# First feed-forward in three rounded parts, in halves of 256 rows, with its weights split on chip

## What the kernel must compute

```python
x = x + _L0_xattn_ref(_layernorm(x), ctx, w_in, b_in, w_out, b_out, w_ct, b_ct, 64)  # banded, 8 heads of 8
x = x + _L0_ffn_ref(_layernorm(x), w_r, b_r, w1, b1, w2, b2)
x = x + _L1_xattn_ref(_layernorm(x), ctx, ctx, Wq, Wk, Wv, Wfc, bfc)                 # 32 heads, 8 key groups
x = x + _L1_ffn_ref(_layernorm(x), gate_w, up_w, down_w, expert_weight, ln_gamma, ln_beta)

def _L0_ffn_ref(x, w_r, b_r, w1, b1, w2, b2):        # the part that is changed
    scores = einsum('bld,d->bl', x, w_r) + b_r
    _, idx = top_k(scores, l // 2)                   # the better half of each sequence's rows
    x_sel = take_along_axis(x, idx[:, :, None], axis=1)
    h = gelu(einsum('bkd,df->bkf', x_sel, w1) + b1)  # 256 -> 1024
    out_sel = einsum('bkf,fd->bkd', h, w2) + b2      # 1024 -> 256
    return zeros_like(x).at[batch, idx].set(out_sel)
```

## Time and profile before

| | |
|---|---|
| time, 3 runs | 342.03 us median (340.19 to 342.74) |
| the profiled execution | 341.85 us, span of the trace 340.1 us |
| busy share of the span | PE 92%, PEld 71%, DVE 70%, ACT 59%, POOL 53% |
| tile 7 of the banded attention | 138.75 to 153.70 us |
| first feed-forward, first half of rows, and last row choice | 164.20 to 185.46 us |
| second half, up to the first score pair | 185.46 to 207.45 us |
| granted PE clock in these stages | 1.00 of the full 2.4 GHz |

### The profile page before, as it was taken

One profiled execution on the slowest core, in us unless ns is written; L12 is line 12 of the kernel. 1 busy time (PEld: TensorE's weight loads), 2 busy tenths in 40 slices (PEclk: granted clock), 3 DMA queues, 4 the chain that ended last, 5 costly groups with the idle time before them and its releaser, 6 DMA issues.

```text
span 340.1 us, 7216 instructions
## 1 busy us (share of the span) xinstructions
PE 312.5 (92%) x2178; PEld 242.9 (71%) x2178; DVE 237.7 (70%) x921; ACT 199.9 (59%) x415; POOL 181.1 (53%) x294
## 2 busy tenths in 40 slices
PE   6978999999999999999998998869899999999993
PEld 5877667767676767765587886657567678888892
DVE  7878888999999998984426256754788746661264
ACT  4648887878787778768540324465768963113210
POOL 6648565677777856576604513343342822335643
PEclk9999999999999999999999999989999999999997
DMA  7999020201010101100000000000000000000000
GB/s 200 369 368 318 3 48 2 49 1 48 3 41 8 33 18 27 26 0 4 2 0 0 2 0 0 2 0 1 2 1 2 0 2 0 3 31 15 18 31 31
DMA packets 13301, 14.51 MB, mean 43 GB/s; under 512 B 2512, under 2 KB 11984, under 8 KB 13264
## 3 DMA queue, kind: packets, MB, share of 16 engines
q1 hardware_dynamic: 12688, 13.72, 12.9%
q10 hardware_dynamic: 576, 0.33, 0.3%
HBM read 10.64 MB, written 1.05 MB: 34 GB/s over the span
## 4 chain that ended last, share of the span: by engine, by line
PE 63%; DVE 16%; issue 8%; ACT 7%; POOL 5%; POOLq 0%; DVEq 0%; ACTq 0%
PE S L421 6%; PE S L761 6%; PE O L448 5%; PE ST L432 4%; DVE masked L1283 4%; PE ST L786 4%; PE S L555 4%; PE S L637 2%; PE S L704 2%; PE PJ L681 2%; PE O L718 2%; PE O L586 2%; PE PJ L394 2%; PE PJ L384 2%; PE XB L693 2%
## 5 line engine op out<-in xcount | busy, mean ns | idle before, releaser
L1283 DVE CUSTOM_DVE_ANT_0 masked<-S,band 128x192 bf16<-128x192 f32 x256 | 80.4, 354 | 12.7 <-PE S L421 11.6
L882 ACT ACTIVATE ex<-ST 128x384 f32<-128x384 f32 x128 | 61.4, 490 | 13.5 <-PE ST L432 11.8
L1067 POOL TENSOR_SCALAR rstd<-mv 128x1 f32<-128x1 f32 x40 | 12.0, 301 | 80.0 <-DVE mv L1220 79.9
L421 PE MATMUL S<-qk 128*128 128x384 f32 x128 | 53.2, 416 | 0.2
L432 PE MATMUL ST<-qk 128*128 128x192 f32 x256 | 47.7, 269 | 2.1 <-ACT ex L882 1.8
L432 PEld LDWEIGHTS ST<-qk 128*128 128x128 f32 x256 | 44.9, 189 | 4.4 <-issue 3.4
L421 PEld LDWEIGHTS S<-qk 128*128 128x128 f32 x128 | 24.1, 188 | 17.9 <-issue 16.1
L1127 POOL TENSOR_SCALAR_AFFINE_SELECT ex<-ex 128x512 f32<-128x512 f32 x32 | 21.3, 665 | 29.0 <-ACT ex L882 28.9
L448 PE MATMUL O<-ex,v 128*32 128x192 f32 x512 | 34.1, 338 | 0.0
L1414 DVE TENSOR_REDUCE mw<-S 128x8 f32<-128x512 f32 x32 | 22.0, 686 | 14.6 <-PE S L637 14.5
L852 ACT ACTIVATE hs<-PJ,sb,byhead 128x512 fp32r<-128x512 f32 x29 | 22.6, 779 | 12.4 <-PE PJ L385 12.0
(11 more groups left out here) (204 smaller groups left out, 720.7 us busy)
## 6 DMA issues: line engine op xcount, KB each, us to landing
qk<-kp SPq DMA_DIRECT2D x48, 48.0 KB
w<-in_w SPq DMA_DIRECT2D x2, 1024.0 KB, 9.8
cx<-in_cx SPq DMA_DIRECT2D x1, 1024.0 KB, 9.0
up<-in_up SPq DMA_DIRECT2D x1, 1024.0 KB, 12.3
down<-in_down SPq DMA_DIRECT2D x1, 1024.0 KB, 11.9
out<-x SPq DMA_DIRECT2D x8, 128.0 KB, 1.7
cxT<-in_cxT SPq DMA_DIRECT2D x1, 768.0 KB, 6.0
x<-in_x SPq DMA_DIRECT2D x1, 768.0 KB, 7.7
```

The source lines that it names most:

```text
L421: mm(out, r32(qp[:, t % 2, g, b, P * c:P * c + P]), r32(mv_), start=True, stop=True).then_inc(s["pe_s"], 1)
L882: A(ex[:, (n // 2) % 4, 2 * w:2 * w + 2, :], ST[n % 2][:, 0:2 * WIN].rearrange("p (h k) -> p h k", h=2), ACT.Exp, scale=SCALE).then_inc(s[ ...
L1283: last = V.tensor_tensor_reduce(out=masked[:, n % 2, h, :], in0=S[n % 2][:, WIN * h:WIN * h + WIN], in1=band[:, c, :], scale=1.0, scalar=N ...
```

## The change

The first feed-forward is computed in three rounded parts as well. For that:

- `w1` and `w2` are split on chip into a rounded part (ACT copy) and a rest (DVE subtraction), in four quarters each: w1 beside tile 7 into a new tile `w1s`, w2 beside tile 7 and in the slots e = 2, 3, 13 and 14 into the room of old keys (`w2s`).
- The gathered rows are split: the first half by one copy and one subtraction beside tile 7, the second half at each take by one more ACT copy and a DVE subtraction (`x_part`).
- An up block is six rounded products in place of two float32 ones; a down block is six for both groups of 128 rows in place of one float32 product for each. After gelu ACT writes the rounded block and DVE the rest (`ffn_low`) into a ring of four blocks; ACT waits for the down block four before.
- Order: one block's products per slot. First half: ups at e = 11, 12, 13, 14, 16, 18, 20, 22, downs at e = 15, 17, 19, 21, 23 to 26. Second half: ups at e = 31 to 38, downs at e = 34 to 41. Scatters 0 to 7 at e = 28, 30, 43 and 44, two each, in banks ST0 and ST1.
- The second layer's slot n now runs with e = n + 47, so its first two slots share e = 29 and 30 with the banded program. The exponential table is loaded at n = -6.
- The tiles `up` and `down` are gone: SP loads the second feed-forward's weights into `w1` and `w2` once those are split.

```diff
@@ loads (SP)
-                    (up[:, :, :], a["up"].rearrange("(k p) f -> p k f", p=P)),
-                    (down[:, :, :], a["down"].rearrange("(k p) f -> p k f", p=P)),
...
+            sp.wait_ge(s["f_w1"], 4)
+            load(w1[:, :, :], a["up"].rearrange("(k p) f -> p k f", p=P), "ld_up")
+            sp.wait_ge(s["f_w2"], 4)
+            load(w2[:, :, :], a["down"].rearrange("(k p) f -> p k f", p=P), "ld_down")
@@ slots
-        SCATTER1 = {-15: (2,), -14: (3,), -3: (4,), -2: (5,), 4: (6, 7)}
+        SCATTER = {28: (0, 1), 30: (2, 3), 43: (4, 5), 44: (6, 7)}
+        UP0, DOWN0 = (11, 12, 13, 14, 16, 18, 20, 22), (15, 17, 19, 21, 23, 24, 25, 26)
...
+        def tail_up(e):
+            if 31 <= e < 31 + FC:
+                return 1, e - 31
+            return (0, UP0.index(e)) if e in UP0 else None
+        def tail_down(e):
+            if 34 <= e < 34 + FC:
+                return 1, e - 34
+            return (0, DOWN0.index(e)) if e in DOWN0 else None
...
+        AHEAD = 47
@@ PE
+            def feed_forward(e):
+                if tail_up(e):
+                    ffn_up(*tail_up(e))
+                if tail_down(e):
+                    ffn_down(*tail_down(e))
+            def ffn_up(g, f):
+                m = FC * g + f
+                if m == 0:
...
+                    pe.wait_ge(s["f_w1"], 4)
                 if f == 0:
-                    pe.wait_ge(s["fa_x"], 4 * half + 4)
+                    pe.wait_ge(s["f_xl"], 4 * g + 1)
                 if m >= 2:
                     pe.wait_ge(s["fa_up"], m - 1)
-                for k in range(2):
-                    last = mm(up_bank(f), w1[:, k, P * f:P * f + P], xsT[:, k, T * half:T * half + T], start=(k == 0), stop=(k == 1))
+                for i, (k, a, b) in enumerate(PARTS):
+                    last = mm(up_bank(f), r32(w1s[:, a, k, P * f:P * f + P]), r32(x_part(g, b)[:, k, :]),
+                              start=(i == 0), stop=(i == len(PARTS) - 1))
...
+            def ffn_down(g, f):
...
+                if g == 0:
+                    pe.wait_ge(s["f_w2"], f // 2 + 1)
+                pe.wait_ge(s["f_lo"], FC * g + f + 1)
+                for m in range(2):
+                    for i, (a, b) in enumerate(((0, 0), (1, 0), (0, 1))):
+                        last = mm(down_bank(2 * g + m), r32(ffn_h(f, a)[:, P * m:P * m + P]), r32(w2s[:, f, b, :]),
+                                  start=(f == 0 and i == 0), stop=(f == FC - 1 and i == 2))
...
+            def slot1(n):
+                e = n + AHEAD
+                if e > 30:
+                    feed_forward(e)
+                    for t in SCATTER.get(e, ()):
+                        scatter(t)
@@ ACT
+                    if t >= 4:
...
+                        last = A(r32(x_part(1, 0)[:, :, o:o + 64]), MT[:, P:2 * P].rearrange("p (k c) -> p k c", k=2), ACT.Copy)
...
+                if T_ == 7 and l in (4, 6, 8, 10):
...
+                    nc.scalar.copy(r32(w1s[:, 0, k, 512 * c:512 * c + 512]), w1[:, k, 512 * c:512 * c + 512]).then_inc(s["f_w1h"], 1)
+                i = {(7, 12): 0, (7, 14): 1, (8, 12): 2, (8, 13): 3}.get((T_, l))
...
+                    nc.scalar.copy(r32(w2s[:, 2 * i:2 * i + 2, 0, :]), w2[:, 2 * i:2 * i + 2, :]).then_inc(s["f_w2h"], 1)
+                if (T_, l) == (7, 2):
...
+                    nc.scalar.copy(r32(x_part(0, 0)), xsT[:, :, 0:T]).then_inc(s["f_xh"], 1)
+            def gelu(g, f):
...
+                A(hT[:, f, 0:T], up_bank(f), ACT.Gelu_apprx_tanh, bias=b1[:, f:f + 1]).then_inc(s["fa_up"], 1)
+                if m >= 4:
+                    act.wait_ge(*ring_last(m))
...
+                A(r32(ffn_h(f, 0)), hT[:, f, 0:T], ACT.Copy).then_inc(s["fa_hi"], 1)
@@ DVE
+                for t in SCATTER.get(e - 1, ()):
+                    ffn_add(t)
+                if e == 27:
+                    ffn_out(0)
+                    ffn_out(1)
...
+                    V.tensor_tensor(r32(x_part(1, 1)[:, :, o:o + 64]), xsT[:, :, 64 * t:64 * t + 64],
+                                    x_part(1, 0)[:, :, o:o + 64], ALU.subtract).then_inc(s["f_xl"], 1)
+                if (T_, l) == (7, 3):
+                    dve.wait_ge(s["f_xh"], 1)
+                    V.tensor_tensor(r32(x_part(0, 1)), xsT[:, :, 0:T], x_part(0, 0), ALU.subtract).then_inc(s["f_xl"], 1)
+                if T_ == 7 and l in (6, 8, 12, 15):
...
+                    V.tensor_tensor(r32(w1s[:, 1, k, cs]), w1[:, k, cs], w1s[:, 0, k, cs], ALU.subtract).then_inc(s["f_w1"], 1)
+                if e in (2, 3, 13, 14):
...
+                    V.tensor_tensor(r32(w2s[:, 2 * i:2 * i + 2, 1, :]), w2[:, 2 * i:2 * i + 2, :], w2s[:, 2 * i:2 * i + 2, 0, :], ALU.subtract)\
+                        .then_inc(s["f_w2"], 1)
+                if tail_up(e - 1):
+                    ffn_low(*tail_up(e - 1))
+            def ffn_low(g, f):
+                dve.wait_ge(s["fa_hi"], FC * g + f + 1)
+                V.tensor_tensor(r32(ffn_h(f, 1)), hT[:, f, 0:T], ffn_h(f, 0), ALU.subtract).then_inc(s["f_lo"], 1)
```

More of the change, by code:

```diff
@@ L94, in build @@
         wf1 = sb("wf1", [P, 2, T])
-        up = sb("up", [P, 2, DF])
-        down = sb("down", [P, FC, T])
+        w1s = sb("w1s", [P, 2, 2, DF])
         eg = sb("eg", [P, 2, T + NEXP])
@@ L397, in slot_ @@
             def slot_(T_, l):
[L398 to L402, removed]
+                feed_forward(since_end(T_, l))
                 t, r = T_, l
@@ L564, in ffn_down @@
                     pe.wait_ge(s["f_x"], 4)
[L565 to L570, removed]
-            def scatter(t):
[L573 to L579, removed]
+                if g == 0:
+                    pe.wait_ge(s["f_w2"], f // 2 + 1)
@@ L594, in _ @@
             warm_up(3)
[L595 to L607, removed]
-            def slot1(n):
[L611 to L614, removed]
-                if i is not None:
-                    ffn_down(1, 0, 2 * i)
-                    ffn_down(1, 0, 2 * i + 1)
-                f = at(n, -4, 1, FC)
-                if f is not None:
-                    ffn_down(1, 1, f)
-                for t in SCATTER1.get(n, ()):
-                    scatter(t)
+            def slot1(n):
+                e = n + AHEAD
+                if e > 30:
+                    feed_forward(e)
+                    for t in SCATTER.get(e, ()):
+                        scatter(t)
                 u = at(n, 0, 1, 4 * TILES)
@@ L785, in moe_down @@
                         pe.wait_ge(s["hpool_up" if half else "h_up"], f + 1)
-                    last = mm(ST[t % 2][:, 0:T], hT[:, f, P * m:P * m + P], down[:, f, :], start=(f == 0), stop=(f == FC - 1))
+                    last = mm(ST[t % 2][:, 0:T], hT[:, f, P * m:P * m + P], w2[:, f, :], start=(f == 0), stop=(f == FC - 1))
                 if f1 == FC:
                     last.then_inc(s["hp_dn"], 1)
-            for n in SLOTS1:
+            ctx_keys(0, 0)
+            for T_, l in SLOTS_ALL:
+                if T_ == 1 and l == 0:
+                    pe.wait_ge(s["ld_rest"], 64)
+                    pe.wait_ge(s["ga_k"], PAIRS)
+                    mm(XB[:, 0:1], wo0[:, :], bcol[:, 0:1], start=True, stop=True).then_inc(s["pe_bias"], 1)
+                if T_ == 1 and l == 4:
+                    pe.wait_ge(s["dve_w"], 4)
+                    pe.wait_ge(s["act_regroup"], 1)
+                    mm(XB[:, 0:P], regroup, wo0[:, :], start=True, stop=True).then_inc(s["pe_wo"], 1)
+                if T_ == 1 and l == 10:
+                    pe.wait_ge(s["act_wo"], 1)
+                slot_(T_, l)
+                if since_end(T_, l) - AHEAD in SLOTS1:
+                    slot1(since_end(T_, l) - AHEAD)
+            for n in SLOTS1[since_end(*SLOTS_ALL[-1]) - AHEAD + 1 - SLOTS1[0]:]:
                 slot1(n)
@@ L945, in _ @@
                            ident[:, 0:96].rearrange("p (r j d) -> p j r d", r=3, j=4)).then_inc(s["act_part"], 1)
-            for T_, l in SLOTS_ALL:
-                slot_(T_, l)
             def slot1(n):
-                f = at(n, -16, 1, FC)
-                if f is not None:
-                    if f == 0:
-                        act.wait_ge(s["fp_x"], TILES)
-                    gelu(1, f)
-                if n == 2:
+                if n + AHEAD > 30 and tail_up(n + AHEAD):
+                    gelu(*tail_up(n + AHEAD))
+                if n == -6:
                     A(warm[:, :], ident[:, 0:1], ACT.Exp)
@@ L1392, in ffn_add @@
                 V.tensor_tensor(x[:, t, :], scatter_bank(t), x[:, t, :], ALU.add).then_inc(s["f_x"], 1)
-            for T_, l in SLOTS_ALL:
-                slot_(T_, l)
             def slot1(n):
-                c = at(n, -4, 8, 2)
-                if c is not None:
-                    ffn_out(2 + c)
+                e = n + AHEAD
+                if e > 30:
+                    if tail_up(e - 1):
+                        ffn_low(*tail_up(e - 1))
+                    if e == 42:
+                        ffn_out(2)
+                        ffn_out(3)
```

(5 more changed lines are left out.)

119 lines of the change are left out of this document (79 added, 40 removed).

## The result

The change took 343.92 us (median of 12 runs, 342.44 to 346.79) against 342.07 us for the kernel before on the same chip; the ratio is 1.0082, 95% interval 1.0054 to 1.0110. The forecast was 343.8 us. The traced execution took 343.33 us, with a span of 341.6 us.

A forecast was written before the change was run, and what follows sets the result against it. TensorE carries 63% of the path, VectorE 16%, with little room in tile 7. Terms +2.6 + 0.1 + 0.3 + 0.4 - 1.5 = +1.9 on the profiled 341.85 us gave 343.8; own range 341 to 346, overall 338.0 to 347.5.

The forecast's parts named there:

- Part 1: Splits beside tile 7: five DVE subtractions exceed DVE's idle time and collide with POOL's selects; +2.6 us (0 to 5).
- Part 2: First half of the first feed-forward, until the gated product: 9.6 us of groups against 9.4; +0.1 (-1 to +1.2).
- The w2 subtractions: At e = 2, 3, 13, 14 in the banded tail, where DVE is 3.89 busy of 10.50: 0, at most 0.6 each.
- ACT's copies: Seven copies of 512 beside tile 7, 4.3 us against 4.13 idle: covered, but with nothing left.
- Parts 2 and 4: Feed-forward's first half, +0.1, and second half up to the first score pair, 12.8 us of groups against 12.2, +0.4.
- Part 3: Last gather, 177.50 to 185.46: a chain through DVE, POOL, PE, ACT gains a copy and a subtraction; +0.3 (-0.3 to +1).
- Part 5: First five score intervals of the second attention: downs, scatters and a 2.99 interval go, 8.76 to 7.3; -1.5 (-2.2 to -0.5).
- I am wrong if: Refuted if tile 7 keeps its length, the second half shrinks over 2 us, or stages after n = 5 move.
- Rival A: Tile 7: every subtraction meets a whole select, +4.4, and +1 for late V products and exponentials; 346.7 us; chance 0.25.
- B: Feed-forward: rounded groups stream at 0.72 and tile 7's floor is absorbed in the banded tail; -3.7, 338.3 us; chance 0.2.
- C: Rounded products no cheaper because weight loads don't hide, 36 us against 27.5; some +10, 352 us; chance 0.03.

The follow-up runs named there:

- ACT cut: The change with ACT's seven rounding copies beside tile 7 cut to 8 columns (4 for x and w2), DVE subtractions whole: 343.81 us, ratio to before 1.0056.
- late w2: The change with only w2's subtractions moved, from e = 2, 3, 13, 14 to e = 13, 14, 20, 21: 341.39 us, ratio to before 1.0014.
- filled waits: The change with subtractions moved, plus seven float32 products in score-slot waits and three each ahead of the spreads at e = 27 and n = 10: 339.07 us, ratio 0.9971.
- float32 in the new order: The change's order and slots with float32 products and no splits: 341.87 us, ratio to before 1.0038.
- the second set of the change: The changed kernel itself, unaltered, run again beside two later kernels on one chip: 343.75 us, ratio to before 1.0068.
- the kernel with placed subtractions: The change with subtractions moved only: two w1 quarters to e = 9, 10, x to slot 15, w2 to e = 13, 14, 20, 21: 341.78 us, ratio to before 1.0010.

## Why the prediction came out

The time was right, in good part by luck: the sum holds for another reason than the one given. Four terms came out 0.2 to 0.4 too high, 1.3 us together, and the clock, which stood in no term, put 1.0 back. The table has each stage in the traced executions, and (third column) its length at full clock, from the kernel named that has the change's instructions there. "Rest" is everything between the fifth score interval and the second feed-forward.

| stage, us | before | after | full clock | forecast | by instructions |
|---|---|---|---|---|---|
| tile 7 to up | 25.48 | 28.44 | 27.78 (ACT cut) | +2.6 | +2.3 |
| first up to last gated | 13.87 | 14.37 | 13.57 (ACT cut) | +0.1 | -0.3 |
| gated to second half | 7.37 | 7.71 | 7.71 | +0.3 | +0.3 |
| second half | 21.99 | 21.97 | 21.97 | +0.4 | 0.0 |
| five intervals | 8.76 | 7.67 | 7.03 (late w2) | -1.5 | -1.7 |
| rest | 57.28 | 56.20 | 55.56 (late w2) | 0 | 0 |

The instructions of the change cost 2.3 - 0.3 + 0.3 + 0.0 - 1.7 = +0.6 us, not +1.9. The clock does the remainder: after, 0.66 + 0.80 us at 165 and 0.64 + 0.64 at 213, 2.7 in all; before, 1.7 at 227. So +0.6 + 2.7 - 1.7 = +1.6, against a measured difference of spans of 1.5 in these two executions. Over all runs with a listed clock the medians are 0.995 (96 runs of before) and 0.980 (24 of the change). Runs at 0.9945 or more, which leave these stretches out, are a test of the column "by instructions": before 340.08 us (52 runs), late w2 340.12 (3; its stages sum to 0.1 under before), filled waits 338.92 (7; 1.1 under); float32 in the new order fits worse, 341.61 (one run, 1.5 over; its stages give 0.8 over). No run of the change got there, so its +0.6 alone is worked out, not timed.

- **Part 1, size right, place wrong.** I let the subtractions stretch tile 7 through the maxima, by 1.3 to 4.4. From first to last score product it grew by 0.56 (13.95 to 14.51). The w1 subtractions cost PE a wait of 1.37 us for tile 5's addition (0.18 to 0.40 in the four kernels that take them all away or move them all; 1.3 us of the stage, 27.78 to 26.48). The working gives 2.5 where the term has 2.6, and Part 2's gives 0.2 where it has 0.1; the two cancel.
- **Part 1, the failed step: "The w2 subtractions ... lie in DVE's idle time of the banded tail ...: 0".** They cost 0.9 us by instructions (27.78 to 26.85). Moving them alone brought the ratio to before from 1.008 to 1.001 and the median of the clock from 0.980 to 0.988; but the kernel before had 0.995 beside that kernel and 0.990 beside the second set of the change, so how much the clock gained by the move is not shown. I looked at DVE's idle time and not at whose step POOL was doing. The collision that I had priced for tile 7 took place here. The Trainium skill's "SBUF — State Buffer" (Who interferes with whom), cited there, agrees that the two collide. A full block would have cost POOL's step the 0.57 us that DVE's operation still had; it cost 0.43, as in the earlier trace rows DVE lost 0.40 of 0.54, so the measured price is somewhat less.
- **ACT's copies** were covered, as said.
- **Parts 2 and 4:** I took 0.80 for a group of six rounded products, between 0.72 and 0.87. Back to back they took 0.72; in the kernel after, from one PJ/ST pair to the next:

```profile
182.65 0.52 PE L606 MATMUL ST<-qk 128*128 128x256 f32 x3
183.01 0.52 PE L606 MATMUL PJ<-qk 128*128 128x256 f32 x3
183.37 0.52 PE L606 MATMUL ST<-qk 128*128 128x256 f32 x3
```

  so both terms came out 0.4 too high. Float32 products in the same order take 1.3 more in the second half (23.28) and 1.6 more before the last gated product (15.16 against 13.57).
- **Part 3** measured +0.34 for +0.3, **Part 5** -1.7 at full clock for -1.5.
- **The clock was in no term.** I quoted 1.00 for the stages and left before's stretch at 227 out, though it was in the trace. "I am wrong if ... stages after n = 5 ... move": they did, by 1.1 us. It was this stretch going (1.7) and another reaching in from 213 (0.6).
- Rival A's place was wrong as Part 1's was; B's size of 0.72 was right, but its absorbed floor was not; C is out.

What stays open: why some waits of over 1 us are followed by a stretch and others not, and which runs get how many; one execution of each kernel has a trace (two of the change).

## What to carry to other kernels

Before calling an added instruction free in an engine's idle time, look at what the neighbour that shares its memory access does in that slot, and whose chain that step is on. Read PE's waits for what they do to the clock too: a wait that costs little by itself can be followed by microseconds at half rate, so compare runs by their granted clock before explaining a difference of half a percent. Where a wait can't be removed, products into a free bank, short enough to fit inside it, can pay: seven in the score slots raised the median clock from 0.98 to 0.991 and made the stage no longer. Ahead of work that isn't waiting, four cost their whole length, 1.7 us.

## What was not expected of the hardware

The price of a half-clock stretch depends on what it falls on: 1.7 us of the 3.4 at 227, where PE was busy throughout; 0.3 of the 3.4 at 214 in the kernel with placed subtractions (five intervals of 7.31 against 7.03), where PE has waits to give; 1.5 of 3.4 at 165. And w2's subtractions of 0.7 to 0.9 us each, moved by 7 to 11 slots, took the ratio to before from 1.0082 to 1.0014, some 2.3 us, of which stage lengths at full clock explain 0.9; the rest is not traced, and the two kernels did not run side by side.
